# A two-layer decoder on one core: norms divided between VectorE and ScalarE, sums placed earlier, and parts of the softmax shift moved to GpSimd

## The reference

```python
    x = _layernorm(x + _L0_attn_ref(x, ...), axis=-1)            # mamba: selective scan, 256 channels, 16 states
    x = _layernorm(x + _L0_xattn_ref(x, ctx_1024, ...), axis=-1) # 16 query heads of 8, one key and value head
    x = _layernorm(x + _L0_ffn_ref(x, ...), axis=-1)             # a shared expert of width 512, 15 routed ones, 3 chosen
    x = _layernorm(x + _L1_attn_ref(x, ...), axis=-1)            # 16 heads of 8, LoRA on queries and values
    x = _layernorm(x + _L1_xattn_ref(ctx_1024, ctx_1024, x, ...), axis=-1)  # one head of 128
    x = _layernorm(x + _L1_ffn_ref(x, ...), axis=-1)             # 8 experts, 2 chosen, silu gate
```

## Time and profile before

| what | us |
|---|---|
| median of 3 runs | 1968.11 |
| lowest and highest | 1967.75, 1969.2 |
| the profiled execution's own time | 1968.36 |
| its span in the trace | 1966.7 |
| busy in the span: PE, DVE, ACT, POOL | 1899.7, 1512.5, 1373.9, 135.3 |

### The profile page before, as it was taken

The page is one execution under the profiler, slowest core; times in us unless marked ns, Lnnn a source line. Parts: engine busy times, 40 slices in busy tenths (PEclk is TensorE's granted clock), DMA queues, the critical chain, the costliest instruction groups (busy, mean ns, idle before and its releaser), DMA issues. The chain is left out here.

```text
span 1966.7 us, 36428 instructions
## 1 busy us (share of the span) xinstructions
PE 1899.7 (97%) x14341; PEld 963.7 (49%) x14341; DVE 1512.5 (77%) x2805; ACT 1373.9 (70%) x2483; POOL 135.3 (7%) x115
## 2 busy tenths in 40 slices
PE   5999999999999999999999999999999999999997
PEld 2556544444444444444444444444444445777755
DVE  6878999999999999999999982234688865444334
ACT  5964688888888888888888888432588864444321
POOL 2850000000000000000000000000800000000000
PEclk8999999999999999999999999999899999999999
DMA  6210000000000000000000000232220000000010
GB/s 184 88 52 1 1 1 1 2 1 2 1 1 2 2 1 2 2 1 1 2 1 1 1 1 2 73 112 67 31 44 4 1 1 0 1 1 1 17 30 30
DMA packets 28021, 37.87 MB, mean 19 GB/s; under 512 B 7247, under 2 KB 21679, under 8 KB 27598
## 3 DMA queue, kind: packets, MB, share of 16 engines
q1 hardware_dynamic: 26670, 33.48, 6.2%
q10 hardware_dynamic: 1184, 2.10, 0.3%
HBM read 29.61 MB, written 0.65 MB: 15 GB/s over the span
## 5 line engine op out<-in xcount | busy, mean ns | idle before, releaser
L1166 DVE TENSOR_REDUCE sb_max_partial<-ps_max_ps 128x1 f32<-128x512 f32 (+1 forms) x1664 | 975.5, 661 | 35.1 <-PE ps_max_ps L895 34.6
L1148 ACT ACTIVATE sb_probs<-ps_score_ps 128x512 f32<-128x512 f32 (+1 forms) x1592 | 852.9, 597 | 108.7 <-PE ps_score_ps L1065 62.0
L1065 PE MATMUL ps_score_ps<-sb_q_stack,sb_key_stack 64*128 64x512 f32 x1561 | 566.7, 446 | 4.4 <-ACT sb_probs L1148 3.5
L895 PE MATMUL ps_max_ps<-sb_key_stack,sb_q_stack 64*128 64x512 f32 (+1 forms) x1560 | 555.7, 437 | 0.0
L1038 PE MATMUL ps_acc_ps<-sb_probs,sb_val_ones 128*32 128x256 f32 x6528 | 463.5, 387 | 0.2 <-ACT sb_probs L1148 0.2
L1065 PEld LDWEIGHTS ps_score_ps<-sb_q_stack,sb_key_stack 64*128 64x128 f32 x1561 | 265.0, 183 | 313.7 <-ACT sb_probs L1148 250.6
L895 PEld LDWEIGHTS ps_max_ps<-sb_key_stack,sb_q_stack 64*128 64x128 f32 x1560 | 265.0, 184 | 9.7 <-DVE sb_max_partial L1166 7.5
L1038 PEld LDWEIGHTS ps_acc_ps<-sb_probs,sb_val_ones 128*32 128x32 f32 x6528 | 157.0, 108 | 206.0 <-issue 132.3
L1869 DVE TENSOR_REDUCE sb_s_max_partial<-ps_s_ps 128x1 f32<-128x512 f32 x256 | 157.4, 682 | 27.8 <-PE ps_s_ps L1715 27.8
L1856 ACT ACTIVATE sb_s_probs<-ps_s_ps 128x512 f32<-128x512 f32 x256 | 141.0, 596 | 32.7 <-PE ps_s_ps L1743 24.1
L2103 DVE TENSOR_SCALAR_CACHE_REDUCE sb_x_scores<-ps_x_score_ps 128x1024 f32<-128x1024 f32 (+1 forms) x56 | 62.0, 1110 | 69.3 <-PE ps_x_score_ps L2090 69.3
(11 more groups left out here) (336 smaller groups left out, 1876.3 us busy)
## 6 DMA issues: line engine op xcount, KB each, us to landing
sb_val<-c_rows SPq DMA_DIRECT2D x16, 512.0 KB, 3.7
sb_e_gate_rows<-e_gate_dram SPq DMA_DIRECT2D x15, 512.0 KB, 4.0
sb_e_w<-L_ffn_rW SPq DMA_DIRECT2D x30, 128.0 KB, 2.1
sb_e_w<-L_ffn_W_T SPq DMA_DIRECT2D x24, 128.0 KB, 2.1
sb_ctx_T<-ctx_T SPq DMA_DIRECT2D x1, 1664.0 KB, 8.2
sb_ctx_T<-ctx_T ACTq DMA_DIRECT2D x1, 1538.0 KB, 9.3
sb_key_stack<-sb_key_halves SPq DMA_DIRECT2D x24, 64.0 KB, 2.1
sb_s_key_stack<-sb_s_highs SPq DMA_DIRECT2D x28, 32.0 KB
```

The source lines that it names most:

```text
L895: nc.tensor.matmul(bank((blk, u))[:, 0:n], queries, keys, start=True, stop=True).then_inc(tile_ready, 1)
L1065: nc.tensor.matmul(score_bank(blk, e), keys, queries, start=True, stop=True).then_inc(score_ready, 1)
L1148: nc.scalar.activation(probs[0:n, c % 3, j * HALF:(j + 1) * HALF], score_bank(blk, e)[0:n, :], ACT.Exp).then_inc(exp_done, 1)
L1166: nc.vector.tensor_reduce(partial[:, blk % 2, h, r:r + 1], bank((blk, u))[:, 0:RANGES[r][1]], AX.X, ALU.max).then_inc(tile_used, 1)
```

## The change

- **Norms.** VectorE writes tiles 0 to 3 and copies the first turned half into `x_T`; ScalarE writes tiles 4 to 7 as `Identity` with the reciprocal as scale and a shift (minus mean times reciprocal, one more small VectorE step) as bias, and copies the second half. `aggregate` can be called early: `context_attention` aggregates each tile when it is done, `context_attention1` each pair; only the last ones are left for the end.
- **Borders.** `residual_norm` is gone. `mamba` and `experts1` do their norm in their own block; the projection of `mamba` signals each half, and so does the last expert of `experts1`, whose sums and statistics go by halves.
- **Sums.** `experts0` finishes its last step by halves of the tokens; the copy of the second half adds twice the residual, so that the turned tiles 4 to 7 are normed straight from PSUM. `self_attention` has TensorE put the residual into the projection's PSUM beforehand, by two matmuls with the identity in the last block, and the norm reads PSUM.
- **Shift parts.** For half A VectorE does the reduce alone. Cast and subtraction are done by GpSimd, in `context_attention` for all 16 blocks, in `self_attention` from the fourth on. Half B stays as it was.

```diff
     def normalize(self, dve, link, last, tiles=range(NT)):
...
+        link(self.aggregate(tiles))
         nc.vector.tensor_scalar(self.var[:], self.mv[:, :, 1], EPS, None, ALU.add).then_inc(k.var_ready, 1)
         dve.wait_ge(k.sd_ready, self.n + 1)
         link(nc.vector.reciprocal(self.rstd[:], self.sd[:]))
-        for t in range(NT):
-            nc.vector.tensor_scalar(k.x_tok[:, t, :], self.res[:, t, :], self.mv[:, t, 0:1], self.rstd[:, t:t + 1],
+        nc.vector.scalar_tensor_tensor(out=self.shift[:], in0=self.mv[:, NT // 2:, 0], scalar=-1.0, in1=self.rstd[:, NT // 2:],
+                                       op0=ALU.mult, op1=ALU.mult).then_inc(k.var_ready, 1)
+        for t in range(NT // 2):
+            nc.vector.tensor_scalar(k.x_tok[:, t, :], self.tile(t), self.mv[:, t, 0:1], self.rstd[:, t:t + 1],
                                     ALU.subtract, ALU.mult).then_inc(k.tile_ready, 1)
+        if self.store_to is None:
+            dve.wait_ge(k.turned_ready, 2 * self.n + 1)
+            nc.vector.tensor_copy(k.x_T[:, 0:HALF], self.turned[:, 0:HALF])
 
     def root(self, act):
...
+        act.wait_ge(k.var_ready, 2 * self.n + 2)
+        for t in range(NT // 2, NT):
+            i = t - NT // 2
+            nc.scalar.activation(k.x_tok[:, t, :], self.tile(t), ACT.Identity, bias=self.shift[:, i:i + 1],
+                                 scale=self.rstd[:, t:t + 1]).then_inc(k.late_tile_ready, 1)
...
@@ mamba @@
+                        if s == 1 and t % 4 == 3:
+                            ins.then_inc(out_ready, 1)
+                norm.turn(pe, 5)
...
-        residual_norm(k, "norm0", out_ps, turned=wide(4), awake=5)
...
@@ context_attention, half A @@
+                if half == "A":
+                    if blk > 0:
+                        dve.wait_ge(first_parts, 3 * blk)
+                    nc.vector.tensor_reduce(neg[:, heads], partial[:, blk % 2, heads, :], AX.X, ALU.max, negate=True).then_inc(first_parts, 1)
+                    return
...
+            def part_first(pool, blk):
+
+                if blk >= 2:
+                    pool.wait_ge(shift_turned, 2 * (blk - 2) + 1)
+                part = part2[:, blk % 2, 0:4, :]
+                pool.wait_ge(first_parts, 3 * blk + 1)
+                nc.gpsimd.tensor_copy(part[:, :, 0], neg[:, 0:4]).then_inc(first_parts, 1)
+                pool.wait_ge(first_parts, 3 * blk + 2)
+                nc.gpsimd.tensor_tensor(part[:, :, 1], neg[:, 0:4], part[:, :, 0].bitcast(F32), ALU.subtract).then_inc(first_parts, 1)
...
@@ experts0 @@
+            def last_out(pe):
...
+                for h in range(2):
+                    for f in range(2):
+                        pe.wait_ge(gated, 2 * (step - 2) + f + 1)
+                        ins = nc.tensor.matmul(out_ps[:, h * HALF:(h + 1) * HALF], w2[:, s, f, :], hidden[:, s, f, h * HALF:(h + 1) * HALF],
+                                               start=False, stop=(f == 1), skip_group_check=True)
+                    ins.then_inc(out_done, 1)
...
-                    nc.vector.tensor_copy(total_T[:, HALF:T], out_ps[:, HALF:T]).then_inc(total_copied, 1)
+                    nc.vector.scalar_tensor_tensor(out=total_T[:, HALF:T], in0=k.x_T[:, HALF:T], scalar=2.0, in1=out_ps[:, HALF:T],
+                                                   op0=ALU.mult, op1=ALU.add).then_inc(gated, 1)
...
@@ self_attention @@
+            ON_GPSIMD = 3
...
+                if blk < ON_GPSIMD:
+                    part_first(dve, nc.vector, blk)
...
+            def start_sums(pe, h):
...
+                nc.tensor.matmul(out_ps[:, 4 * h:4 * h + 4, :], k.ident[:], k.x_tok[:, 4 * h:4 * h + 4, :], start=True, stop=False,
+                                 skip_group_check=True)
...
+            SUMS_AT = {7: 0, 11: 1}
...
@@ context_attention1 @@
-                                merge(dve, p - 1)
+                                link(merge(dve, p - 1))
+                                norm.aggregate([2 * p - 2, 2 * p - 1])
...
@@ experts1 @@
-                    add_up(dve, E - 1, 1, E // 2 - 1)
-        residual_norm(k, "norm5", acc, added=True, store=store)
+                    link = k.chain(dve)
+                    dve.wait_ge(added[0], E // 2)
+                    for h in range(2):
+                        dve.wait_ge(out_done, E + h)
+                        for t in range(4 * h, 4 * h + 4):
+                            ins = nc.vector.scalar_tensor_tensor(out=acc[:, t, :], in0=out_ps[:, 1, t, :], scalar=gates[:, t, E - 1:E],
+                                                                 in1=acc[:, t, :], op0=ALU.mult, op1=ALU.add)
+                        link(ins)
+                        for t in range(4 * h, 4 * h + 4):
+                            ins = norm.stats(t)
+                    norm.normalize(dve, link, ins)
```

More of the change, by code:

```diff
@@ L143, in __init__ @@
         self.rstd = k.sb(tag + "_rstd", [P, NT], F32, ctx)
+        self.shift = k.sb(tag + "_shift", [P, NT // 2], F32, ctx)
         self.stored = k.sem("stored") if store is not None else None
@@ L146, in __init__, with tile, aggregate, normalize @@
         k.norms += 1
+    def tile(self, t):
+        return self.res[t // 4][:, t % 4, :] if isinstance(self.res, tuple) else self.res[:, t, :]
     def stats(self, t):
-        return self.k.nc.vector.bn_stats(self.bn[:, t, :], self.res[:, t, :])
-    def normalize(self, dve, link, last):
+        return self.k.nc.vector.bn_stats(self.bn[:, t, :], self.tile(t))
+    def aggregate(self, tiles):
+        for t in tiles:
+            ins = self.k.nc.vector.bn_aggr(self.mv[:, t, :], self.bn[:, t, :])
+        return ins
+    def normalize(self, dve, link, last, tiles=range(NT)):
         k, nc = self.k, self.k.nc
         link(last)
-        for t in range(NT):
-            ins = nc.vector.bn_aggr(self.mv[:, t, :], self.bn[:, t, :])
-        link(ins)
+        link(self.aggregate(tiles))
         nc.vector.tensor_scalar(self.var[:], self.mv[:, :, 1], EPS, None, ALU.add).then_inc(k.var_ready, 1)
@@ L169, in root @@
         if self.store_to is None:
-            for h in range(2):
-                act.wait_ge(k.turned_ready, 2 * self.n + h + 1)
-                nc.scalar.copy(k.x_T[:, h * HALF:(h + 1) * HALF], self.turned[:, h * HALF:(h + 1) * HALF])
+            act.wait_ge(k.turned_ready, 2 * self.n + 2)
+            nc.scalar.copy(k.x_T[:, HALF:T], self.turned[:, HALF:T])
     def turn(self, pe, awake=3):
         k, nc = self.k, self.k.nc
-        for _ in range(awake if self.store_to is None else 0):
+        for _ in range(awake):
@@ L228, in lay_out @@
+        for h, ready in enumerate((k.tile_ready, k.late_tile_ready)):
+            sp.wait_ge(ready, NT // 2 * (self.n + 1))
+            sp.dma_start(self.store_to[:, 4 * h:4 * h + 4, :], k.x_tok[:, 4 * h:4 * h + 4, :]).then_inc(self.stored, 16)
+        sp.wait_ge(self.stored, 32)
 def lay_out(k):
@@ L487, in mamba @@
         out_ps = wide(2).rearrange("p (t e) -> p t e", t=NT)
+        res = k.sb("mamba_res", [P, NT, D], F32, ctx)
+        norm = Norm(k, "norm0", ctx, res, wide(4))
         def half(x, h):
@@ L701, in _ @@
                         drives(m // 2 + 1, range(NT)[FIRST_TILES * (m % 2):FIRST_TILES + NT * (m % 2)])
+                norm.root(act)
             @block.vector
@@ L1267, in _ @@
                         negate(dve, link, blk, "B")
[L1268 to L1270 removed]
+                    for t in range(NT - 1):
+                        link(finish_tile(dve, t))
+                        norm.aggregate([t])
+                    norm.normalize(dve, link, finish_tile(dve, NT - 1), [NT - 1])
     k.layer0.close()
@@ L1486, in _ @@
                     add_b2(pe)
-                    for step in range(2, STEPS):
+                    for step in range(2, STEPS - 1):
                         out(pe, step)
```

196 lines of the change are left out of this document (104 added, 92 removed).

## The result

| what | before | changed |
|---|---|---|
| median, us | 1968.11 | 1955.58 |
| lowest and highest | 1967.75, 1969.2 | 1951.94, 1960.46 |
| the profiled execution's own time | 1968.36 | 1960.46 |
| its span | 1966.7 | 1958.7 |
| busy in the span: PE, DVE, ACT, POOL | 1899.7, 1512.5, 1373.9, 135.3 | 1897.5, 1501.3, 1380.7, 145.6 |

What follows compares the result with a forecast made beforehand. VectorE nearly bounds attention, TensorE and ScalarE set most of the pace; between stages the norm chains count. 7.4 for norms and sums + 2.1 + 4.5 for shift parts = 14.0, so 1968.4 - 14.0 = 1954.4 us, range 1948.5 to 1962.

Steps and rivals of the forecast that it cites:

- Shift parts: Attention borders: VectorE away 0.13 instead of 0.53 us (context) and 0.1 instead of 0.48 (self); saves 2.1 and 4.5 us.
- rival (b): Both attentions: VectorE bounds the stage and all that it saves comes through, 1950.1 us; chance 0.10.
- Norm tails: Five norms that turn: tiles shared by VectorE and ScalarE, 2.7 instead of 3.15 us, 0.45 each, 2.2 in all.
- Mamba's sums: After mamba's projection: first sum starts at its first half, 138.0 instead of 139.22, so statistics end 1.2 us earlier.
- The experts of layer 0: Their last step: VectorE's idle 0.82 us and the second sum (0.67) go, the copy grows by 0.06; saves 1.4 us.
- Early aggregation: Context and layer-1 attention: seven and six of eight tiles are aggregated before the end; saves 0.55 and 0.5 us.
- The last sums: Last stage: four sums fit into VectorE's 1.32 us of idle time before the last expert's sums; saves 1.4 us.
- Second store: Last stage: tiles shared by two engines bring the second of SP's two stores about 0.55 us forward.
- Self-attention sums: Self attention: two sums leave the tail, 1.35 us; two identity matmuls cost 1.8 in the last block; a loss of 0.45.
- (a): Borders inside attention pay nothing: TensorE and ScalarE set the pace, or GpSimd holds VectorE up; 1961.0 us; chance 0.17.
- (d): Attention borders: GpSimd's pair outlasts 3.1 us and each border loses the excess; 1980 us at 4 us; chance 0.04.
- (c): Behind norms, TensorE's clock: one half-speed stretch more or less, about 3 us either way, 1951 or 1957; chance 0.07.

Runs made afterwards that it cites:

- e1: Changed kernel with cast and subtraction of the first halves back on VectorE in both attentions: 1964.7 us, ratio 0.9972.
- e8: Changed kernel with the division of the norms undone, VectorE writing all eight tiles and ScalarE copying both halves: 1957.37 us, ratio 0.9951.
- e3: Changed kernel with the two identity matmuls moved from self attention's last block into gaps of its tail: 1952.69 us, ratio 0.9914.
- e4: Changed kernel with five tiles by VectorE and three by ScalarE in the four norms that read SBUF: 1955.82 us, ratio 0.9927.
- e2: Changed kernel with VectorE's casts in self attention replaced by a sum with itself times zero: 1952.99 us, ratio 0.9912.
- the two profiles: Profiled executions of the unedited changed kernel, the first and one from a later repetition: spans 1958.7 and 1950.7 us; medians 1955.58 and 1951.87.
- e6: Changed kernel with a sum for VectorE's casts in self attention and GpSimd's pair held back by ten memsets from the fourth block: 2016.12 us, ratio 1.0238.

## Why the prediction was right, point by point

The two causes that carry the forecast, shorter chains between the stages and a VectorE that is away from its maxima for less time, were both found where it put them. The shift parts (e1), the division of the norms (e8) and the place of the identity matmuls (e3) were each undone or moved by an edit. The gains at the borders of mamba and the experts, from early aggregation and in the last stage are read from stretches of the traces alone.

- **Shift parts**, forecast 2.1 and 4.5. The mechanism and the sizes held: 1.85 from the first to the last exponential of context attention and 0.37 ahead of them, 5.1 over the 13 blocks of self attention. "0.35 a border" was 0.39, so nearly everything that VectorE saves there comes through (towards rival (b)). In context attention 0.14 of 0.40 comes through; there the waits of one block add up to 2.1 us of VectorE waiting for TensorE, 1.8 in before. GpSimd's steps are 0.19 and 0.20, against 0.23 taken from the earlier trace rows.
- **Norm tails**, forecast 0.45 each, 2.2. Measured 0.30, 0.31, 0.45, 0.27 and 0.30 at full clock: 1.6. The mis-sized term is ScalarE's tile, taken as 0.243 from start to start by the earlier trace rows; it is 0.39 from SBUF, so one of the prediction's own signs of being wrong (tiles that take 0.4 each) came out. The copies of the earlier trace rows have a scale only and read PSUM; these tiles have a bias as well. The source makes little of the difference: in the norms after the experts of layer 0 and after self attention these tiles read PSUM too, and are 0.35 apart. The 0.10 that is left goes with the bias or with something else that differs; the bias was not tried alone. The Trainium skill (ScalarE: Activation LUTs, Rules for kernel authors) budgets about 0.3 us an activation and 0.83 ns an element, by estimate 0.41 a tile. The sum by that page, half a microsecond smaller, is about what came. Yet in e4 ScalarE's last tile ended 0.38 us earlier and the tail shrank by 0.07 only: the turn of the second half, one tile after the other on TensorE, comes next, as the prediction's "0.4 more" had it.
- **Awake matmuls.** The forecast let the turn start with the first tile. In the norm after context attention at half clock it does not; that norm and the merge ahead of it lost 0.5 instead of gaining 1.0.
- **Sums and borders.** Mamba's sums were put at 1.2 and brought 1.1 (3.02 us from the projection's end to the epsilon step, 4.13 in before). The experts of layer 0 were put at 1.4 and brought 1.6. Early aggregation, 0.55 and 0.5, brought 0.46 (4.69 us from the last exponential to the epsilon step in e2, at full clock, against 5.15) and 0.4. The last sums, 1.4, brought 1.43.
- **Second store** 0.55: 0.04. ScalarE's last tile lets SP's second issue end 0.29 earlier, and what follows it took 2.57 instead of 2.32 us; that the two stores, closer together, share the queues is one reading and not shown.
- **Self-attention sums** -0.45: -0.84. The tail's part is 1.37 (1.35 forecast); the two matmuls cost 2.21, not 1.8.
- Together 5.8 for the norms (7.4 forecast) and 7.3 for the parts (6.6): 13.1 against 14.0. This takes the norm after context attention at full clock, as e2 has it; with the tails that the two profiles have it is 11.9 and 12.4. The rest of each measured difference lies in stretches without a term, where half clock and the meeting of cast and sum fell against the change in the first profile, and where the change came out ahead in the second.
- **Rivals.** (a) fell with e1, (d)'s price with e6. (c) named the right mechanism and a fair size: with the meeting of cast and sum it makes most of the difference between the two profiles. What the forecast missed altogether is in its sentence that GpSimd's "fills and its sum come before the fourth block": true, and so for the third block, which stayed on VectorE, the cast can meet that sum. The earlier trace rows showed the cast's 0.99 beside a memset of 0.95; it was read as a danger of the moved steps, and not asked of those that stayed.

## What to carry to other kernels

A step handed to an idle engine paid here about what the waiting engine was held up: look for the wait that it ends (0.41 us, and the blocks got 0.39 shorter), then for when the result is fetched (2.1 us later). After shortening a chain, look at what was parked beside it as harmless: matmuls that keep an engine awake, a long GpSimd sum, a cast whose neighbour has moved by one microsecond. Price a stall of TensorE with the half-clock stretch that can follow it; in ten of thirteen blocks of e6 that cost as much again or more.

## What the runs showed of the hardware that was not expected

- A 128x4 cast on VectorE waited for the GpSimd instruction at work (1.95 beside a 2.37 sum, 0.17 alone), and in six cases for one that started up to 0.07 us after it (0.99 to 1.04, all of a memset of 0.95). The subtraction (0.16) and the sum that rounds (0.16) didn't wait for memsets. The Trainium skill (SBUF — State Buffer, Who interferes with whom) says that casts can enter a mode that takes the port shared with GpSimd, one engine blocking the other for a whole instruction; these rows agree.
- In e6 2 us of TensorE waiting at a border were followed by a granted clock of 0.50 in ten of thirteen blocks, and such a block lost 4.5 us.
- VectorE's 128x128 tile takes 0.34 us from SBUF and 0.40 from PSUM; ScalarE's 0.48 and 0.46.
